# Pair counts of a graph kept in f16, and two of twelve count scatters per attention round held back in SBUF

## The reference

```
h = relu(layernorm(x)); x = x + L0(h)   # two graph attentions: softmax over the edges of each dst, sum of h[src], ELU, linear
h = relu(layernorm(x)); x = x + L1(h)   # five rounds: agg = segment_sum(norm * (h[src] + edge_fea), dst), linear, batch norm
h = relu(layernorm(x)); x = x + L2(h)   # hW = h @ W + b; out = segment_sum(hW[dst], src) / deg(src)
h = relu(layernorm(x)); x = x + L3(h)   # edge MLP, segment_sum by src, GRU
```

## Time and profile before

| | us |
|---|---|
| median of 3 runs | 4242.43 (4240.96 to 4242.7) |
| the profiled execution | 4242.47 |
| its span | 4240.6 |

### The profile page before, as it was taken

The page is one execution under the profiler, slowest core; times in us unless marked ns, Lnnn a source line. Parts: engine busy times, 40 slices in busy tenths (PEclk is TensorE's granted clock), DMA queues, the critical chain, the costliest instruction groups (busy, mean ns, idle before and its releaser), DMA issues. The chain is left out here.

```text
span 4240.6 us, 63598 instructions
## 1 busy us (share of the span) xinstructions
PE 3481.7 (82%) x15628; PEld 2329.0 (55%) x15629; DVE 2453.7 (58%) x7750; ACT 1046.0 (25%) x2509; POOL 2138.7 (50%) x1892
## 2 busy tenths in 40 slices
PE   6276777887777777645999999999959799999988
PEld 4145555555555555432555555555545567777754
DVE  7756777777777777645212121212155467777768
ACT  0121222222222222112303031313144323333322
POOL 0356888887878878600777771000000056666610
PEclk9987777777777777776999999999969899999999
DMA  9358555655556665581554544232213144444420
GB/s 394 96 134 288 132 141 135 139 136 135 138 132 141 133 136 134 110 182 28 171 175 147 178 148 124 86 114 83 82 35 116 66 107 113 114 113 115 114 63 22
DMA packets 494780, 546.18 MB, mean 129 GB/s; under 512 B 226047, under 2 KB 396509, under 8 KB 493803
## 3 DMA queue, kind: packets, MB, share of 16 engines
q0 software_dynamic: 142864, 256.80, 25.2%
q1 hardware_dynamic: 339118, 268.48, 21.6%
q10 hardware_dynamic: 12749, 20.33, 1.3%
HBM read 474.83 MB, written 111.55 MB: 138 GB/s over the span
## 5 line engine op out<-in xcount | busy, mean ns | idle before, releaser
L1038 PE MATMUL p_out<-rows,hot 128*128 128x266 f32 x2048 | 817.6, 554 | 31.0 <-DVE rows L1160 23.1
L963 POOL DMA_INDIRECT count_dram<-number,place x384 | 650.6, 1694 | 159.0 <-issue 111.8
L1038 PEld LDWEIGHTS p_out<-rows,hot 128*128 128x128 f32 x2048 | 517.1, 272 | 224.3 <-DVE rows L1160 120.4
L955 POOL DMA_INDIRECT rows<-att_dram,idx x512 | 552.1, 1078 | 163.0 <-issue 128.2
L1506 PE MATMUL p_lo<-cbuf,parts 128*128 128x400 f16 x1750 | 582.2, 333 | 0.0
L1507 PE MATMUL p_hi<-cbuf,parts 128*128 128x400 f16 x1750 | 581.8, 332 | 0.0
L2075 POOL DMA_INDIRECT col_rows<-col_dram,m_idx x440 | 416.5, 947 | 281.2 <-ACT m_idx L2145 170.0
L1575 POOL DMA_INDIRECT rec_dram<-records,edge_place x416 | 403.3, 969 | 131.4 <-issue 126.4
L1535 DVE TENSOR_TENSOR node_sum<-p_hi,low_sb 128x400 f32<-128x400 f32 x80 | 45.9, 574 | 650.0 <-ACT low_sb L1526 650.0
L1978 POOL MEMSET attr_w<- 128x512 f32 x1 | 0.5, 526 | 781.9 <-POOLq L364 781.9
L1160 DVE TENSOR_TENSOR rows<-rows 128x512 f32<-128x512 f32 x512 | 349.3, 683 | 0.2 <-ACT rows L929 0.2
(11 more groups left out here) (391 smaller groups left out, 6175.4 us busy)
## 6 DMA issues: line engine op xcount, KB each, us to landing
cbuf<-by_src SPq DMA_DIRECT2D x40, 2500.0 KB
count_dram<-zeros SPq DMA_DIRECT2D x40, 1000.0 KB, 23.3
dl_rep<-dl_dram SPq DMA_DIRECT2D x128, 256.0 KB
by_src<-count_dram POOLq DMA_DIRECT2D x25, 800.0 KB, 49.7
g_rows<-by_src SPq DMA_DIRECT2D x25, 800.0 KB, 4.3
rec_dram<-blank ACTq DMA_DIRECT2D x1, 17600.0 KB
records<-in_edges POOLq DMA_DIRECT2D x32, 520.0 KB, 4.1
key_rep<-key_dram SPq DMA_DIRECT2D x64, 256.0 KB
```

Source lines behind the costliest of these rows:

```text
L955: nc.gpsimd.indirect_dma_start(rows[r][:, u, :], None, att_dram, bass.IndirectOffsetOnAxis(ap=idx[r][:, u:u + 1].bitcast(U32), axis=0)).th ...
L963: nc.gpsimd.indirect_dma_start(count_dram, bass.IndirectOffsetOnAxis(ap=place[r][:, n, c:c + 1].bitcast(U32), axis=0), number[r][:, 2 * n ...
L1038: m = nc.tensor.matmul(p_out[q][:, side, 0:HALF], hot[k][:, u, :], rows[k][:, u, side * HALF:(side + 1) * HALF], start=(u == 0), stop=(u = ...
```

## The change

- `count_dram`, `zeros` and all `number` tiles are f16. `by_src` is no tensor of its own but a view of `count_dram`; the cast and its semaphore are gone. The fill is 20 DMAs of 4000 elements a partition.
- `LATE` is -256 (up to 255 equal keys add to -65280, and the largest f16 is 65504): a number above 0 is a count, one of 0 or below marks a later edge.
- In attention each round still computes 12 chunks. Ten are scattered (`IN_LOOP`): 4 in the first group, 2 in each of the others. The second pair of the third group is copied, numbers and places, to `number_post` and `place_post`.
- The 32 pairs kept so (64 scatters) go out later, each pair waiting for all before it: 27 in the unify stage, 5 in the set-up stage of L1, where GpSimd then waits until all have landed.

```diff
+FIRSTS = (0, 4, 6, 8)
+IN_LOOP = 10
+POST = 2 * (GROUPS // 4)
+POST_UNIFY = 27
-LATE = 1024.0
+LATE = -256.0
-ZF = 2000
+ZF = 4000
+        place_post = sb("place_post", [P, POST // 2, 2], I32)
+        number_post = sb("number_post", [P, POST // 2, 2], F16)
-        zeros = sb("zeros", [P, ZF], F32, early)
+        zeros = sb("zeros", [P, ZF], F16, early)
-        number_pre = sb("number_pre", [P, PRE], F32, early)
+        number_pre = sb("number_pre", [P, PRE], F16, early)
-        count_dram = dram("count_dram", [KD + TRASH, 1], F32)
+        count_dram = dram("count_dram", [KD + TRASH, 1], F16)
-        by_src = dram("by_src", [NP, NP], F16)
+        by_src = count_dram[0:KD, :].rearrange("(p n) o -> p (n o)", p=NP)
+        def scatter_late(pool, first, last):
+            for n in range(first, last):
+                pool.wait_ge(placed, (CH - POST + 2 * n) * 16)
+                pool.nop().then_inc(waits_passed, 1)
+                for c in range(2):
+                    nc.gpsimd.indirect_dma_start(
+                        count_dram, bass.IndirectOffsetOnAxis(ap=place_post[:, n, c:c + 1].bitcast(U32), axis=0),
+                        number_post[:, n, c:c + 1], None, compute_op=ALU.add).then_inc(placed, 16)
...
-                number = [sb(f"number{r}", [P, 4], F32, inner) for r in range(4)]
+                number = [sb(f"number{r}", [P, 4], F16, inner) for r in range(4)]
...
-                            r, before = (k + 3) % 4, i * BODY + PRE + PARTS[k][0]
+                            r, before = (k + 3) % 4, i * IN_LOOP + PRE + FIRSTS[k]
-                            if k % 2 == 0:
+                            if k == 0:
                                 pair(k, 0, before)
...
-                                if k % 2 == 0:
+                                if k == 0:
                                     gather(r, 1)
-                            if k % 2 == 0:
+                            if k == 0:
                                 pair(k, 1, before + 2)
                             else:
                                 pair(k, 0, before)
...
-                        pool.wait_ge(placed, CH * 16)
+                        pool.wait_ge(placed, (CH - POST) * 16)
...
-                                dve.wait_ge(placed, i * (BODY * 16) + (PRE + first + count - BODY) * 16)
+                                dve.wait_ge(placed, i * (IN_LOOP * 16) + (PRE + FIRSTS[k] + (4 if k == 0 else 2) - IN_LOOP) * 16)
...
-                        def at_place(k):
-                            n = PARTS[k][1] // 2
+                        def at_place(k, i):
+                            n = 2 if k == 0 else 1
+                            if k == 2:
+                                late = number_post[:, bass.ds(i, 1), :].rearrange("p o c -> p (o c)")
+                                TT(late, number[k][:, 2:4], number[k][:, 2:4], ALU.max)
+                                TT(place_post[:, bass.ds(i, 1), :], place_f[:, 1:2, :], own_place[:].unsqueeze(1), ALU.add)
                             TT(place[k][:, 0:n, :], place_f[:, 0:n, :], own_place[:].unsqueeze(1).broadcast_to([P, n, 2]),
                                ALU.add).then_inc(place_ready, 1)
...
-                        for t in range(NT):
-                            pool.dma_start(by_src[t * P:(t + 1) * P, :], counts[t * P:(t + 1) * P, :]).then_inc(narrowed, 16)
-                        pool.wait_ge(narrowed, 16 * NT)
+                        scatter_late(pool, 0, POST_UNIFY)
...
+                @block.gpsimd
+                def _(pool):
+                    scatter_late(pool, POST_UNIFY, POST // 2)
+                    pool.wait_ge(placed, CH * 16)
```

More of the change, by code:

```diff
@@ L36 @@
 BODY = 12
+FIRSTS = (0, 4, 6, 8)
+IN_LOOP = 10
+POST = 2 * (GROUPS // 4)
+POST_UNIFY = 27
 PRE = 32
 PRE_PLAN, PRE_WEIGHTS = 3, 5
-LATE = 1024.0
+LATE = -256.0
 PRESENT = 2.0 ** 100
 PER = 12
-assert KP * KB == CH and PRE + BODY * (GROUPS // 4) == CH and 2 * P < LATE
+assert KP * KB == CH and PRE + BODY * (GROUPS // 4) == CH and 2 * P <= -LATE and (2 * P - 1) * -LATE < 65504
 HJ = 425
@@ L623, in _ @@
                     o.need(n)
-                    o.link(nc.vector.scalar_tensor_tensor(pre_f[:], number_pre[:], LATE, key_off[:, 0:PRE // 2, :].rearrange("p n c -> p (n c)"),
-                                                          ALU.is_lt, ALU.mult))
+                    o.link(nc.vector.scalar_tensor_tensor(pre_f[:], number_pre[:], 0.0, key_off[:, 0:PRE // 2, :].rearrange("p n c -> p (n c)"),
+                                                          ALU.is_gt, ALU.mult))
                     TT(place_pre[:].rearrange("p (n c) -> p n c", c=2), pre_f[:].rearrange("p (n c) -> p n c", c=2),
@@ L1139, in if_first @@
                             dve.wait_ge(keys_used, g + 1)
-                            return STT(place_f[:, 0:n // 2, :].rearrange("p n c -> p (n c)"), number[k][:, 0:n], LATE,
+                            return STT(place_f[:, 0:n // 2, :].rearrange("p n c -> p (n c)"), number[k][:, 0:n], 0.0,
                                        key_off[:, bass.ds(i * (BODY // 2) + (PRE + first) // 2, n // 2), :].rearrange("p n c -> p (n c)"),
-                                       ALU.is_lt, ALU.mult)
-                        def at_place(k):
-                            n = PARTS[k][1] // 2
+                                       ALU.is_gt, ALU.mult)
+                        def at_place(k, i):
[4 more added lines that the diff above has]
+                                TT(place_post[:, bass.ds(i, 1), :], place_f[:, 1:2, :], own_place[:].unsqueeze(1), ALU.add)
                             TT(place[k][:, 0:n, :], place_f[:, 0:n, :], own_place[:].unsqueeze(1).broadcast_to([P, n, 2]),
@@ L1230, in work @@
                             o.need(n)
-                            at_place(k1)
+                            at_place(k1, i1)
                             assert o.n == PER
@@ L1248, in _ @@
                         o.link(if_first(0, 0, 0))
-                        at_place(0)
+                        at_place(0, 0)
                         o.begin(PER)
@@ L1284, in program @@
                 fold_in, fold_ready, fold_taken = sem("c_fold_in"), sem("c_fold_ready"), sem("c_fold_taken")
-                narrowed = sem("c_narrowed")
                 c_order, neg_ready, exp_ready, elu_ready, val_turned, valT_ready, uni_ready, x_added = (
@@ L1301, in _ @@
                     def _(pool):
-                        counts = count_dram[0:KD, :].rearrange("(n f) o -> n (f o)", f=NP)
-                        for t in range(NT):
-                            pool.dma_start(by_src[t * P:(t + 1) * P, :], counts[t * P:(t + 1) * P, :]).then_inc(narrowed, 16)
-                        pool.wait_ge(narrowed, 16 * NT)
+                        scatter_late(pool, 0, POST_UNIFY)
                     @block.vector
```

## The result

The changed kernel took 4228.91 us (median of 8 runs, 4225.67 to 4233.91), the kernel before on the same chip 4242.47 (8 runs, 4236.14 to 4246.05): ratio 0.9971, 95% interval 0.996 to 0.9982. It is faster, by 13.6 us; 26.9 were forecast. The profiled execution took 4227.34 us, its span is 4225.4, 15.2 shorter than before. That is where the stages are compared. The change-over is the time from the end of DVE's copy of `F_sb`, its last work in attention, to its first work in unify. A DMA has landed when the engine that waits for its semaphore can go on.

The account below looks back on a forecast made before the run. In attention, GpSimd was taken as full, with the ring of PE and DVE as the floor at 11.56 us a group. Terms -25 - 5.9 + 4 = -26.9 took 4242.4 to 4215.5 us; own range 4205 to 4226, wide range 4203 to 4241.

Parts of the forecast that it names:

- Two scatters of twelve leave the round: Attention: GpSimd's round of four groups shrinks by 4.0 us; 25 us gained, bounds 0 and 28.6.
- The ring: Attention: the loop of DVE and PE work once per group, said to set a floor of 11.56 us a group.
- the two added DVE operations: Attention, behind the third group's place: about 0.33 us in all, covered by DVE's wait for p_tab, cost 0.
- The zero fill halves: First and planning stages: 20 fills instead of 40; 5.9 us gained together, bounds 3 and 7.3.
- The memset by elements: First stage: GpSimd's memset of zeros, priced by elements, delays DVE by 1.4 us; priced by bytes, 0.
- the wait for the first keys: Planning stage: DVE's 1.95 us wait for a broadcast queued behind the fill goes; 2.0 us gained.
- The cast goes: Unify stage: its 25 DMAs were hidden, so removing them gives 0, up to 1 us if bandwidth was shared.
- 27 pairs in unify: Unify stage: late scatter pairs 6.03 us apart stay hidden with 18 us to spare, cost 0.
- rival (a): f16 scatter-adds land late, 7.8 us a pair, lengthening unify and set-up; 4248 us, slower; chance 0.09.
- Five pairs in the set-up stage: Set-up of L1: late pairs and SP's 4-byte writes hold each other up; cost 4 us, bounds 0 and 12.
- rival (d): End of attention: GpSimd's wait for its last scatters may have a share; up to 6 us more gained, 4209; chance 0.07.
- Everything behind: After the set-up stage: chunks and row tiles are read from the same layout, same bytes; 0.

## Why the prediction was wrong

The direction was right, and the wide range (4203 to 4241) held the time, but the forecast's own (4205 to 4226) did not; the gain was half of what was forecast. Against the forecast's 26.9 us the span shows 15.2, so 11.7 are missing. By its steps:

- *Two scatters of twelve leave the round*, -25: measured -25.6. The ring as the floor held (11.52 us a group for 11.56), and so did hiding the two added DVE operations. The waits for scores fell by 28.2 us, as the forecast had them. The forecast gave all of the gain to the scatters left out and took f16 as free of effect on the loop; in one profile each, those alone gave 14.3 and f16 alone 10.5. Part of the match may be luck.
- *The zero fill halves*, -5.9: measured -4.85. The memset by elements held. The first stage gave 4.3 (forecast 3.9), the planning and score stages 0.55 (forecast 2.0), though the wait for the first keys did go.
- *The cast goes*, 0, and *27 pairs in unify*, 0: the stage grew by 1.25 us, which is not the pairs' doing (182.6 us without them). Pairs are 5.8 us apart, so rival (a), a dearer f16 scatter-add everywhere, fell.
- ***Five pairs in the set-up stage* is the step that failed: "I take +4, which is three pairs at 1.3 us of mutual delay each". Measured +11.3.** No row had that 1.3 us, and there is no such delay pair by pair: the first pair was waited for 13.1 us, the second 5.15, the others 2.2. Its upper bound, "+12 (the first pair lands only with dinv at 2003, four periods behind it)", was the mechanism, and it had been set aside although the row for it was there: a 12.5 KB write that took 17.5 us. I read that row as a slow transfer. The runs showed that it is a late landing: packets over within 8 us, landing after 16, and the scatters that land beside it held too. 30 pairs in unify give back 11.5 of it, rows of 512 bytes 9.5.
- *Behind attention*, costed at 0 with rival (d) for up to 6 us better: it was 5.6 worse, 3.7 of it in the change-over. GpSimd's wait did have a share, as (d) supposed; what it waited for was not seen. (DVE is idle for 0.6 to 1.7 us at the other change-overs of the kernel before, not 1.2 to 1.5.) The landing of the padded last chunk costs 10.5 us more in f16 here (21.3 for 10.8 us from the last scatter's end to unify), while GpSimd is through 9.9 us before DVE's copy ends in place of 3.1, which takes back 6.8. The remaining 1.9 goes with TensorE's granted clock. The last p_out took 6.72 us at a granted clock of 0.56, in place of 5.51 at 0.69 (1.00 is 2.4 GHz, and 0.5 would be 1.2). In three kernels it ran at 1.00 in 3.83 us, and the stretch from p_in 128 to the end of the copy took 19.8 to 20.0 us; in the twelve where it ran at 0.55 or 0.56 that stretch took 22.8 to 23.8. Why the clock stood where it did stays open.
- *Everything behind*, 0: -3.0 in this profile, but 2220.2 to 2225.2 in all kernels, so a spread and no effect. Without it 14.7 us would be missing.

The Trainium skill (DMA: Bandwidth & Descriptors, "Specifications") says that pieces under 512 bytes make the DMA engine read, modify and write. That agrees in direction with 16.1 us for dinv's 4-byte pieces against 1.35 for 512-byte ones, but the size alone does not make the delay: ordinary scatters of 2-byte elements are waited for 2.3 us. The Trainium skill (the same page, "Anatomy of one DMA — SWDGE (gpsimd) path") says of DMAs issued by GpSimd that the semaphore waits for the confirmation that the last byte has landed, most of a fixed 2 us, and that this can be surprisingly long for HBM, the chip's DRAM. The 2.3 us agree, and the 17.7 of the padded chunk, with the DMA engines idle, fit a late confirmation, though no trace shows it apart. That spacing small places 64 bytes apart removes the delay is shown by the runs here alone.

## What to carry to other kernels

Look for waits on a landing with all DMA engines idle. Here they marked small neighbouring writes: the padding of a last chunk that goes to a dense trash area, a vector written element by element. Spread such places, or turn the vector first; before hiding work behind such a write, ask what else has to land beside it, because that work can inherit its delay.

When a bound of the estimate is a mechanism whose row is already in the profile, price that mechanism and don't split the difference.

## What the runs showed of the hardware

- A scatter-add of 128 elements with some 122 of them in neighbouring 2-byte places was waited for 17.7 us after its issue ended, with 4-byte places 6.3; with places 64 or 128 bytes apart it landed early enough that DVE was last. In the long wait no DMA engine was busy beyond the first 3 us.
- That delay is passed on: scatters issued beside dinv's write were waited for 7.5 us (in attention), 13.1 to 16.2 (in set-up, five kernels) and 20.0 (in unify), against 2.3 in unify without it and 5.2 to 6.6 beside SP's other loads of the set-up stage.
- For the trash places only the spacing (and with it the size of the area) was changed, so the dense places are the cause there; for dinv both size and number of pieces changed, and the two causes were not separated.
- A GpSimd memset took time by elements, not bytes: 4000 of 2 bytes 3.43 us, 2000 of 4 bytes 1.76.
- The same 16 matmuls of the last p_out took 3.83 us at a granted TensorE clock of 1.00 and 6.7 to 6.9 at 0.55 to 0.56.
